# Graph attention and edge network on one core: four consecutive nodes to a partition, one head scatter a group

## The reference, cut to what matters

```python
# layer 1: graph attention, 4 heads of 64
x_proj = x @ lin_W.T                                  # [50000, 256]
att = s_src[src] + s_dst[dst] + s_edge                # s_* : 4 numbers a node or edge
att = where(att >= 0, att, 0.2 * att)
exps = exp(att - segment_max(att, dst)[dst])          # edges and self loops
out = segment_sum(x_proj[src] * exps / denom[dst], dst)
x = layernorm(x + out + bias)
# layer 2: an edge network
h = tanh(concat(x[src], x[dst]) @ W0 + b0)
h = tanh(h @ W1 + b1) @ W2 + b2
h = h * (edge_attr_128 @ Wg)
x = layernorm(x + segment_mean(h, src))
```

## Time and profile before

| what | value |
|---|---|
| runs | 5044.54 us median of 3 (5033.79 to 5050.71) |
| profiled execution | span 5498.8 us, 87081 instructions |
| PE busy | 4252.2 us, 77% of the span |
| DVE busy | 3806.6 us, 69% |
| POOL busy | 3300.0 us, 60% |
| ACT busy | 3248.7 us, 59% |
| DMA | 975.10 MB, mean 177 GB/s |

### The profile page before, as it was taken

The page is one execution under the profiler, slowest core; times in us unless marked ns, Lnnn a source line. Parts: engine busy times, 40 slices in busy tenths (PEclk is TensorE's granted clock), DMA queues, the critical chain, the costliest instruction groups (busy, mean ns, idle before and its releaser), DMA issues. The chain is left out here.

```text
span 5498.8 us, 87081 instructions
## 1 busy us (share of the span) xinstructions
PE 4252.2 (77%) x24476; PEld 3420.0 (62%) x24476; DVE 3806.6 (69%) x12195; ACT 3248.7 (59%) x7255; POOL 3300.0 (60%) x3036
## 2 busy tenths in 40 slices
PE   6777777777657776599999997889989999999500
PEld 3455545555434444599999995777777777777400
DVE  7766666666656665798989875666666666666564
ACT  7755555555533343366666665666666676666575
POOL 0255555555666665455555546777777888888532
PEclk9999999999977887799999998999999999999755
DMA  3232322323275555699999995666666666666596
GB/s 82 55 86 80 87 80 81 88 80 84 71 150 166 166 165 166 221 368 354 367 353 365 355 322 139 143 141 145 144 150 139 146 149 148 147 151 145 144 394 275
DMA packets 774331, 975.10 MB, mean 177 GB/s; under 512 B 182069, under 2 KB 685148, under 8 KB 761084
## 3 DMA queue, kind: packets, MB, share of 16 engines
q0 software_dynamic: 170176, 323.19, 26.3%
q10 hardware_dynamic: 269085, 374.19, 18.9%
q1 hardware_dynamic: 334715, 273.49, 16.5%
HBM read 541.99 MB, written 429.16 MB: 177 GB/s over the span
## 5 line engine op out<-in xcount | busy, mean ns | idle before, releaser
L1381 PE MATMUL bank<-w0r,n_x1T 128*128 128x406 f32 x4704 | 905.8, 352 | 36.1 <-issue 16.9
L1381 PEld LDWEIGHTS bank<-w0r,n_x1T 128*128 128x128 f32 x4704 | 870.4, 190 | 59.9 <-ACT n_pa L1429 35.3
L1528 POOL DMA_INDIRECT out_x<-u_sums,u_row x392 | 639.5, 1631 | 143.8 <-issue 116.8
L580 POOL DMA_INDIRECT DS<-by_dst,rank_int x392 | 376.0, 959 | 572.8 <-DVE rank_int L750 427.8
L1580 PE MATMUL bank<-u_h,w1r 128*108 128x512 f32 (+1 forms) x2646 | 680.0, 401 | 0.0
L406 PEld LDWEIGHTS bank<-wst,xT 128*128 128x128 f32 x2352 | 332.2, 201 | 430.1 <-issue 311.4
L406 PE MATMUL bank<-wst,xT 128*128 128x264 f32 x2352 | 409.5, 312 | 242.6 <-DVE xps L415 196.8
L832 POOL DMA_INDIRECT xg<-XP,m_src x392 | 420.3, 1072 | 222.7 <-DVE msg L892 113.5
L1257 POOL DMA_INDIRECT n_cg<-CT,n_last x392 | 445.8, 1137 | 175.3 <-issue 95.2
L1510 POOL DMA_INDIRECT u_pa<-PA,u_rows x392 | 408.5, 1042 | 202.1 <-issue 111.1
L1580 PEld LDWEIGHTS bank<-u_h,w1r 128*108 128x108 f32 (+1 forms) x2646 | 436.6, 172 | 127.1
(11 more groups left out here) (286 smaller groups left out, 10637.8 us busy)
## 6 DMA issues: line engine op xcount, KB each, us to landing
PA<-n_pa ACTq DMA_DIRECT2D x98, 816.0 KB
PB<-n_pb ACTq DMA_DIRECT2D x98, 812.0 KB
XP<-xps ACTq DMA_DIRECT2D x98, 528.0 KB
CT<-ct ACTq DMA_DIRECT2D x98, 528.0 KB
n_xp<-XP SPq DMA_DIRECT2D x98, 528.0 KB
xin<-in_x SPq DMA_DIRECT2D x97, 512.0 KB
n_x<-in_x SPq DMA_DIRECT2D x97, 512.0 KB
out_x<-n_x ACTq DMA_DIRECT2D x97, 512.0 KB, 4.8
```

The source lines that it names most:

```text
L580: pool.indirect_dma_start(out=DS, out_offset=bass.IndirectOffsetOnAxis(ap=ri[s][:, j:j + 1], axis=0), in_=pd[s][:, j, :], in_offset=None). ...
L1381: o = nc.tensor.matmul(acc, xT[s][p][:, k, e], w0r[q][:, 2 * half + k, :], start=(n == 0), stop=(n == len(terms) - 1))
L1528: pool.indirect_dma_start(out=out, out_offset=bass.IndirectOffsetOnAxis(ap=si[s][:, j:j + 1], axis=0), in_=yo[s][:, j, :], in_offset=None, ...
```

## The change

Node n = 512 g + 4 p + t now sits in partition p, tile 4 g + t: four consecutive nodes to a partition. `nodes(a, g)` is the new view, four rows of a partition in one run. LO and HI are split accordingly, and the prefix sums run over the 98 groups and, within a quad of four nodes, over its four. All loads and stores of node tables in stages 2 and 5 take the new view; nothing changes in stages 6 and 7.

The head scatter: one for each group in place of four. It puts the 16 words of s_dst of four nodes (and a word -FAR) in the row of the quad's first edge, at word 8 of DS, whose rows grow from 16 to 25 words. The payload's words 6 and 7, zero before, now hold the quad's number and the node's place in it. ACT also stores the 16 words of each quad to a new table SD, from which `f0` is gathered.

In the messages s_dst is spread by a scan over 64 partitions (4 tiles x 4 nodes x 4 heads), with a reset that comes from word 24 of the row, and then masked by "the edge's node is this one of the four" (`node_in_quad`); the product that adds s_dst to the logits sums over the quad (`gather4`).

```diff
+    def nodes(a, g):
+        return a[bass.ds(g * (G * P), G * P), :].rearrange("(p t) w -> p t w", t=G)
...
-    DW = 16
+    QW = G * HEADS
+    HEAD = 8
+    DW = HEAD + QW + 1
...
+    SD = nc.dram_tensor("SD", (NP // G, QW), f32, kind="Internal").ap()
...
+                        pool.wait_ge(h_pad, 3)
+                        nc.gpsimd.memset(far[:].rearrange("p (r w) -> p r w", w=DW)[:, :, DW - 1:DW], 0.0).then_inc(h_pad, 1)
...
+                        c.step(nc.vector.tensor_scalar(ki[1][:], KI[:, 0, 0:NT], 2, None, ALU.arith_shift_right))
+                        c.did(nc.vector.tensor_copy(PD[:, :, 6], ki[1][:]))
+                        c.did(nc.vector.tensor_copy(PD[:, :, 7], ki[4][:]))
...
-                        c.step(nc.vector.tensor_scalar(tot[1][:], hist[:], 0.0, OOB, ALU.is_equal, ALU.mult))
-                        c.did(nc.vector.tensor_tensor(heads[:], tot[1][:], start[:], ALU.add))
+                        c.step(nc.vector.tensor_scalar(none[:], quad[:], 0.0, OOB, ALU.is_equal, ALU.mult))
+                        c.did(nc.vector.tensor_tensor(heads[:], none[:], cum[:], ALU.add))
...
-                            for j in range(G):
-                                pool.indirect_dma_start(
-                                    out=DS, out_offset=bass.IndirectOffsetOnAxis(ap=hx[s][:, j:j + 1], axis=0),
-                                    element_offset=8, in_=sn[s][:, j, :], in_offset=None,
-                                    bounds_check=NP - 1, oob_is_err=False).then_inc(ds_st[s], 16)
+                            pool.indirect_dma_start(
+                                out=DS, out_offset=bass.IndirectOffsetOnAxis(ap=heads[:, g:g + 1], axis=0),
+                                element_offset=HEAD, in_=sn[s][:], in_offset=None,
+                                bounds_check=NP - 1, oob_is_err=False).then_inc(ds_st[s], 16)
...
-                            nc.scalar.copy(sn[s][:], xps[s][:, :, D + HEADS:XW]).then_inc(sd_ok, 1)
-                            act.dma_start(tiles(XP, g), xps[s][:]).then_inc(xp_stored[s], 16)
+                            nc.scalar.copy(sn[s][:, 0:QW].rearrange("p (t h) -> p t h", t=G), xps[s][:, :, D + HEADS:XW])\
+                                .then_inc(sd_ok, 1)
+                            act.dma_start(nodes(XP, g), xps[s][:]).then_inc(xp_stored[s], 16)
+                            act.wait_ge(sd_ok, g + 1)
+                            act.dma_start(SD[g * P:(g + 1) * P, :], sn[s][:, 0:QW]).then_inc(xp_stored[s], 16)
...
-                            nc.vector.tensor_copy(hx[s][:], heads[:, t4])
...
-                        sp.dma_start(ds[:, bass.ds(g * G, G), :], tiles(DS, g)[:, :, 0:12]).then_inc(ds_ld[s], 16)
+                        sp.dma_start(ds[:, bass.ds(g * G, G), :], tiles(DS, g)).then_inc(ds_ld[s], 16)
...
-                        c.step(nc.vector.tensor_tensor(rf[s][:, 1:P], k[:, 0, 0:P - 1], k[:, 0, 1:P], ALU.subtract))
-                        nc.vector.tensor_tensor_scan(sd[s][:], rf[s][:, 0:P], k[:, 1, :], -BIG, ALU.add, ALU.max)\
-                            .then_inc(m_em, 1)
+                        c.did(nc.vector.tensor_tensor_scan(sq[s][:], k[:, 1, :], QB[0:TQ, 2 * P:3 * P], -BIG,
+                                                           ALU.add, ALU.max))
+                        c.did(nc.vector.tensor_tensor(rf[s][:, 1:P], k[0:TH, 0, 0:P - 1], k[0:TH, 0, 1:P], ALU.subtract))
+                        c.wait()
+                        nc.vector.scalar_tensor_tensor(sd[s][:], QB[0:TQ, 3 * P:4 * P], node_in_quad[0:TQ], sq[s][:],
+                                                       ALU.is_equal, ALU.mult).then_inc(m_em, 1)
...
-                        nc.tensor.transpose(LT[0:TH, 0:P], ks[s][:].rearrange("p t h -> p (t h)"), ident[:])
-                        nc.tensor.transpose(LT[0:TH, P:2 * P], sh[s][:].rearrange("p t h -> p (t h)"), ident[:])\
-                            .then_inc(m_lt, 1)
+                        nc.tensor.transpose(QB[0:TQ, 0:P], ks[s][:].rearrange("p t h -> p (t h)"), ident[:])
+                        for k, b in enumerate((1, 2, 0)):
+                            o = nc.tensor.transpose(QB[0:TQ, (1 + k) * P:(2 + k) * P],
+                                                    tq[s][:, b].rearrange("p t w -> p (t w)"), ident[:])
+                        o.then_inc(m_lt, 1)
...
-                        nc.tensor.matmul(LT[0:TH, 0:P], ident[0:TH, 0:TH], sd[s][:], start=False, stop=True).then_inc(m_lt, 1)
+                        nc.tensor.matmul(LT[0:TH, 0:P], gather4[0:TQ, :], sd[s][:], start=False, stop=True).then_inc(m_lt, 1)
...
-                        nc.scalar.copy(sh[s][:], ds[:, bass.ds(g * G, G), 8:8 + HEADS]).then_inc(m_ks, 1)
+                        nc.scalar.copy(tq[s][:, 2], ds[:, bass.ds(g * G, G), HEAD:HEAD + QW]).then_inc(m_ks, 1)
+                        nc.scalar.copy(tq[s][:, 0:2], ds[:, bass.ds(g * G, G), HEAD - 1:DW:QW + 1].rearrange("p t k -> p k t")
+                                       .unsqueeze(3).to_broadcast([P, 2, G, QW]))
...
-                        sp.dma_start(xpn[s][:], tiles(XP, g)).then_inc(n_ld[s], 16)
+                        sp.dma_start(xpn[s][:], nodes(XP, g)).then_inc(n_ld[s], 16)
...
-                        act.dma_start(tiles(PA, g), pa[s][:]).then_inc(pa_st[s], 16)
-                        act.dma_start(tiles(PB, g), pb[s][:]).then_inc(pb_st[s], 16)
+                        act.dma_start(nodes(PA, g), pa[s][:]).then_inc(pa_st[s], 16)
+                        act.dma_start(nodes(PB, g), pb[s][:]).then_inc(pb_st[s], 16)
```

More of the change, by code:

```diff
@@ L144, in load_rows, with load_nodes @@
         eng.dma_start(buf[0:TAIL_ROWS, TAIL_TILES, :], a[r0:N, :]).then_inc(sem, 16)
+    def load_nodes(eng, buf, a, g, last, sem):
+        if not last:
+            eng.dma_start(buf[:, :, :], nodes(a, g)).then_inc(sem, 16)
+            return
+        eng.dma_start(buf[0:TAIL_QUADS, :, :], a[(GROUPS - 1) * G * P:N, :].rearrange("(p t) w -> p t w", t=G))\
+            .then_inc(sem, 16)
     top = ExitStack()
@@ L193, in gnn_kernel @@
         krf = [alloc(srt, f"key_rowsf{q}", [P, NC, P]) for q in range(2)]
-        ki = [alloc(srt, f"key_digit{q}", [P, NT], i32) for q in range(4)]
+        ki = [alloc(srt, f"key_digit{q}", [P, NT], i32) for q in range(6)]
         h_pad, h_loaded, h_rows, h_psum, h_chain = (sem("h_pad"), sem("h_loaded"), sem("h_rows"), sem("h_psum"),
@@ L360, in gnn_kernel @@
             xps = [alloc(srt, f"xps{s}", [P, G, XW]) for s in range(2)]
-            sn = [alloc(srt, f"r_s_dst{s}", [P, G, HEADS]) for s in range(2)]
+            sn = [alloc(srt, f"r_s_dst{s}", [P, QW + 1]) for s in range(2)]
             x_loaded, xp_stored = sems("p_x_loaded"), sems("p_xp_stored")
@@ L475, in _ @@
                         pe.wait_ge(h_rows, 3)
-                        nc.tensor.matmul(OB[0][:, 0:NT], ones[:], hist[:], start=True, stop=True)
-                        nc.tensor.matmul(OB[2][:, 0:NT], after[:], hist[:], start=True, stop=True).then_inc(h_psum, 1)
+                        by_quad = hist[:].rearrange("p (g t) -> p g t", t=G)
+                        for t in range(G):
+                            nc.tensor.matmul(OB[0][:, 0:GROUPS], ones[:], by_quad[:, :, t], start=(t == 0), stop=(t == G - 1))
+                        for t in range(G):
+                            o = nc.tensor.matmul(OB[2][:, 0:GROUPS], after[:], by_quad[:, :, t],
+                                                 start=(t == 0), stop=(t == G - 1))
+                        o.then_inc(h_psum, 1)
                     @block.vector
@@ L556, in gnn_kernel @@
                 kcol = [alloc(ph, f"key_col{s}", [P, G]) for s in range(2)]
-                hx = [alloc(ph, f"r_head_rows{s}", [P, G], i32) for s in range(2)]
                 pd = [alloc(ph, f"by_dst{s}", [P, G, 8]) for s in range(2)]
@@ L701, in _ @@
                         c.did(nc.vector.tensor_copy(prior[:, (G - 1) * P:G * P], upto[:]))
+                        for s in range(2):
+                            c.did(nc.vector.memset(sn[s][:, QW:QW + 1], -FAR))
                         def keys(g, s):
@@ L790, in gnn_kernel @@
             rf = [alloc(ph, f"m_reset{s}", [TH, P + 1]) for s in range(2)]
-            sd = [alloc(ph, f"m_s_dst{s}", [TH, P]) for s in range(2)]
+            sq = [alloc(ph, f"m_s_dst_quad{s}", [TQ, P]) for s in range(2)]
+            sd = [alloc(ph, f"m_s_dst{s}", [TQ, P]) for s in range(2)]
             mf = alloc(ph, "m_max_f", [TH, P])
```

117 lines of the change are left out of this document (75 added, 42 removed).

## The result

The kernel after takes 5065.35 us, the median of 5 runs; before, beside it, 5043.2. The ratio is 1.0046, with a 95% interval of 1.003 to 1.0062: 22 us slower, where 4944 was forecast.

What follows compares the result with a forecast made beforehand. POOL's scatters were taken to bound the ranking at 10.2 us a group. Ranking -105, drain -4, messages +8, carry +5 and nodes -5 sum to -101, from 5044.5 to 4944 us; 8-in-10 range 4855 to 5030.

Steps and rivals of the forecast that it cites:

- "remote" waits: Ranking and messages: DVE's 232.7 us of waiting for late PE releases, taken as lost only in the profiled execution.
- sum of floors: Ranking, messages, edges: POOL's needs, 527 us under the profile against 454 for the median; ranking put at 1035 us.
- Next late is DVE: Ranking: with POOL relieved, DVE bounds at 8.9 us a group; 930 us with allowance, from 1035, so -105.
- rival B: Ranking: not set by POOL in plain runs; fewer scatters give 0 to -10, kernel 5080 us; chance 0.11.
- Rival D: Ranking: freed from POOL, but ACT's issue and the projection bank's ping-pong leave 9.9 us a group; 5024 us; chance 0.13.
- ACT's second issue: Ranking: ACT's added DMA issue for the new s_dst table, 0.38 us a group, with ACT at 8.4, under 8.9.
- The drain: End of the ranking: the last group drains three scatters earlier, -4 us.
- Histogram: Histogram stage: larger fill and payload writes against shorter prefix sums, about +2 and -2; 0, within 3 us.
- messages: Messages stage: extra DVE, PE and ACT work mostly covered by POOL's gathers; +8 us, range 0 to 56.
- carry: Carry stage: `own` reads 25 words a row, not 16; +5 us, between 0 and 9.
- Nodes: Nodes stage: PE keeps the pace and the shorter DMAs hide under it; -5 us, between 0 and -40.
- rival C: Nodes: set by the DMA, longer runs move faster; -73 in place of -5, so 4876 us; chance 0.08.

Runs made afterwards that it cites:

- a_evac_early: After, with DVE's projection evacuations for tiles 1, 2 and 3 moved ahead of the equality count and one-hots: 5027.1 us, 0.9961 of before (quiet condition).
- a_no_mask: After, without DVE's masking and the transpose feeding it in the messages: 5248.1 us, 0.9706 of before (slower, holding condition).
- b_again3: The kernel before, unchanged, profiled again in the quiet condition: span 5049.4 us.
- b_heads_in_bounds: Before, its four head scatters taking ranks as row indices so none is out of bounds: 5401.5 us, 0.9992 of before (slower, holding condition).
- b_one_head: Before, with one of a group's four head scatters issued and three left out: 5161.8 us, 0.9536 of before (slower, holding condition).
- a_again: The kernel after, unchanged, run beside before in the slower, holding condition: 5217.95 us, 0.9643 of before.

## Why the prediction was wrong

**Profile and runs.** That 454 us of the profiled execution were missing from the plain runs was right, and the sum of floors led to a ranking of 1035; it took 1030. POOL as its bound, in a chain of 1.26 to 1.30 us, was right too. That "remote" waits belong to the profiled execution was wrong: they belong to the holding condition, and there the plain runs are as long as the profiles.

**Ranking, the step that failed.** "Next late is DVE: 8.9 a group, 872 us", and 930 with an allowance. After took 1005. The one group at 8.9 us that I read the earlier trace rows is the shortest of all in that trace: from one issue of DVE's L750, the group's ranks, to the next it takes 8.89 us, the group behind it takes 20.47, the longest, and the median is 13.15. It gave what DVE can do with its inputs ready, not what the engines keep up together. The ring of 6.8 us of PE and 3.2 us of DVE with the signals between them takes 10.24, by chance the same as POOL's 10.23. So rival B's condition, another engine's need of over 10.2 us a group, held in effect, by a ring and not by an engine: DVE was at 881 of 1005 us and PE at 880. Rival D had the mechanism (the ping-pong of the one projection bank) and priced it at 9.9. Its other suspect, ACT's second issue, did not set the 10.24: in a_evac_early it is still there at 9.82. So the step that failed is the next bound behind POOL: 8.9 a group in the prediction, 10.24 in the run.

**The drain.** -4 forecast. From the last rank to the next stage before takes 32 us and after 13 (both in the quiet condition): -19. POOL had been behind by a backlog and not by three scatters only. The groups themselves gave 6 of the 25 us.

**Histogram, messages, carry.** Within 3 forecast, +4 measured; +8 forecast, -6 measured, with 554 to 564 us in three profiles that have these same messages, so nothing to be told from 0; +5 forecast and +5 measured. POOL's gathers, the cover that was named for the messages, need 418 + 397 x 0.30 = 537 of these 556 us, which fits a cover that held; the one experiment on it (a_no_mask) did not decide.

**Nodes.** -5 (0 to -40) forecast, +37 in the profiles; 23 to 32 us in four comparisons of kernels, 16 in a fifth. The sign was outside the bounds: I let longer runs only help. The Trainium skill (Perfetto Trace Analysis, DMA Optimizations) says that batching transfers of 2 KB or less to 4 or 8 KB can improve throughput much. The packets did get cheaper for their bytes (46 ns for 1024 bytes, 159 for 4096, medians of b_again3 and after), but the rate of the stage, 364 GB/s, did not go up; it fell to 351, so the measurement decides against the gain here. It was rival C's rule, and C is refuted with its sign. Which transfer's length costs the stage stays open. The share of busy DMA did fall below 1 (0.92), as I had written, and meant nothing good.

**The busiest engine.** The Trainium skill (Perfetto Trace Analysis, Identifying the Most-Contended Engine) looks for the highest occupancy. In the quiet condition before's ranking shows DVE at 881 of 1030 us and POOL at 768; yet POOL was the bound, as its 784 x 0.30 us between DMAs are not counted as busy (768 + 235 = 1003). The rule misleads here, where issue gaps are large.

**Slips in the prediction's numbers.** Rival B's "15 to 61" should begin at 13 (8 + 5), and the highest slice of GB/s in the nodes is 368, not 367; neither moves a chance.

So the sum of -101 became +13 between the two profiles of the quiet condition (+22 between medians): ranking and drain had 84 us too much credit (-109 against -25), the nodes 42 too little cost, the messages 14 too much cost, and histogram, edges and final norm add 2.

## What to carry to other kernels

When an engine is relieved, the next bound can be a ring through several engines and one buffer, longer than the busy time of any, as here. Follow one steady group around until it closes, and look at the spread of all groups before you take the speed of one. If a profile and the runs shown differ by 9%, first profile the same kernel again and see whether the runs beside it differ too; compare stages only within one condition. Where one PSUM bank is shared, try moving its consumer to the front of its engine's order: here that gave 40 us of the ranking without less work, and brought up the next wait behind it.

## What the runs showed of the hardware

The same kernel took 5043 to 5047 us in one condition and 5403 to 5414 in another, the difference nearly all in two stages (ranking +265 us, messages +93); the chips numbered 4 and 14 showed both. In the slower one PE's signals came late: in the ranking for 5.2 us around four scatters of 16-byte rows on POOL, in bounds or not (b_heads_in_bounds 0.9992), and for 0.8 us around a single scatter, of 16-byte rows (b_one_head) or of 68-byte rows (a_again). In after and b_again3, both quiet, no signal of the ranking, messages, nodes or edges came over 0.5 us late. In the nodes, runs of 4.1 to 6.5 KB moved 351 GB/s where runs of 1.0 to 1.6 KB moved 364, at a lower busy share (0.92 against 1.00).
